# Third stage of a fused kernel: the outputs' sum and rounded part on GpSimd for two heads at a time, and reciprocals of two score tiles in one instruction

## What is computed

```python
def _L1_attn_ref(x, norm_scale, split_scale, Wq, Wk, Wv, Wo):
    ...
    nrm = jnp.linalg.norm(x, axis=-1, keepdims=True) * d ** (-0.5)
    h = norm_scale * x / (nrm + EPS) * split_scale
    q = (h @ Wq.T).reshape(b, s, H, dh)
    k = (h @ Wk.T).reshape(b, s, G, dh)
    v = (h @ Wv.T).reshape(b, s, G, dh)
    ...
    scores = jnp.einsum('bghsd,bgtd->bghst', q, k) / np.float32(np.sqrt(dh))
    attn = jax.nn.softmax(scores, axis=-1)
    out = jnp.einsum('bghst,bgtd->bghsd', attn, v)
    out = out.reshape(b, H, s, dh).transpose(0, 2, 1, 3).reshape(b, s, H * dh)
    return x + out @ Wo.T
...
x = L0_attn_x
x = x + _layernorm(_L0_attn_ref(_layernorm(x, axis=-1)), axis=-1)
x = x + _layernorm(_L0_ffn_ref(_layernorm(x, axis=-1), L0_ffn_factors, L0_ffn_bias), axis=-1)
x = x + _layernorm(_L1_attn_ref(_layernorm(x, axis=-1), ...), axis=-1)
x = x + _layernorm(_L1_ffn_ref(_layernorm(x, axis=-1), ...), axis=-1)
```

## Time and profile before

| what | value |
|---|---|
| time, median of 3 runs | 1461.83 us (1461.3 to 1461.9) |
| the profiled execution's time | 1460.45 us |
| its span in the profile | 1458.6 us |
| PE busy | 1386.4 us, 95% of the span |
| DVE busy | 1010.8 us, 69% |
| ACT busy | 798.1 us, 55% |
| POOL busy | 740.7 us, 51% |
| mean granted clock of PE | 0.989 |

### The profile page before, as it was taken

The page is one execution under the profiler, slowest core; times in us unless marked ns, Lnnn a source line. Parts: engine busy times, 40 slices in busy tenths (PEclk is TensorE's granted clock), DMA queues, the critical chain, the costliest instruction groups (busy, mean ns, idle before and its releaser), DMA issues.

```text
span 1458.6 us, 20717 instructions
## 1 busy us (share of the span) xinstructions
PE 1386.4 (95%) x6864; PEld 1134.4 (78%) x6864; DVE 1010.8 (69%) x2070; ACT 798.1 (55%) x1554; POOL 740.7 (51%) x1008
## 2 busy tenths in 40 slices
PE   5999999988999999999999999799999999999996
PEld 4888877766777877878787887588888888888884
DVE  5888869867989898989898989666242442434333
ACT  4666646647777878786868788632222222213221
POOL 5888646735536465554646455553343424333241
PEclk9999999999999999999999999999999999999998
DMA  6665133241302112121212041430101011010100
GB/s 192 169 174 127 40 101 116 87 130 38 94 4 64 65 44 88 44 87 37 87 28 96 15 121 40 145 138 1 58 1 59 4 54 58 0 58 0 58 29 29
DMA packets 53516, 101.32 MB, mean 69 GB/s; under 512 B 3760, under 2 KB 4784, under 8 KB 53424
## 3 DMA queue, kind: packets, MB, share of 16 engines
q1 hardware_dynamic: 49728, 92.83, 19.1%
q0 software_dynamic: 3696, 7.34, 3.1%
HBM read 70.79 MB, written 25.17 MB: 66 GB/s over the span
## 4 chain that ended last, share of the span: by engine, by line
PE 75%; DVE 13%; POOL 4%; issue 4%; ACT 3%; DMA 1%; SPq 0%; POOLq 0%; DVEq 0%; ACTq 0%
PE context L1889 13%; PE score L2367 11%; PE context L2367 11%; PE context L58 6%; PE score L58 6%; PE context L2395 5%; PE turned L2395 5%; PE score L899 4%; PE turned L1925 4%; PE context L1951 2%; PE context L1953 2%; DVE g_neg_max L1754 2%; PE context L1925 2%; DVE g_q L1677 1%; DVE g_ptl L1770 1%
## 5 line engine op out<-in xcount | busy, mean ns | idle before, releaser
L1413 POOL TENSOR_SCALAR g_prob<-g_prob,g_inv_sum 128x512 f32<-128x512 f32 x256 | 178.0, 697 | 268.9 <-DVE g_inv_sum L1759 268.8
L1548 ACT ACTIVATE g_prob<-score,g_neg_max 128x512 f32<-128x512 f32 x256 | 177.2, 692 | 115.5 <-DVE g_neg_max L1754 113.1
L2143 POOL TENSOR_TENSOR f_hl<-f_hidden,f_hh 128x512 fp32r<-128x512 f32 x88 | 121.9, 1386 | 216.0 <-DVE f_hh L2276 216.0
L1754 DVE TENSOR_REDUCE g_neg_max<-score 128x1 f32<-128x512 f32 x256 | 174.7, 682 | 43.9 <-PE score L58 43.4
L2367 PE MATMUL context<-g_hth,f_w 128*128 128x512 f32 x352 | 137.8, 391 | 2.3 <-ACT f_w L2193 2.2
L2367 PE MATMUL score<-g_hth,f_w 128*128 128x512 f32 x352 | 137.8, 392 | 0.6 <-DVE g_htl L2293 0.5
L2367 PE MATMUL context<-g_htl,f_w 128*128 128x512 f32 x352 | 137.1, 390 | 0.0
L2367 PE MATMUL score<-g_htl,f_w 128*128 128x512 f32 x352 | 137.1, 390 | 0.0
L58 PE MATMUL score<-g_kh,g_q 128*128 128x512 f32 x256 | 123.4, 482 | 10.7 <-ACT g_prob L1548 7.5
L2199 ACT ACTIVATE f_silu<-score,g_bits 128x512 f32<-128x512 f32 x44 | 30.3, 690 | 176.1 <-PE score L2367 176.1
L2199 ACT ACTIVATE f_silu<-context,g_bits 128x512 f32<-128x512 f32 x44 | 30.4, 690 | 174.5 <-PE context L2367 174.5
(11 more groups left out here) (261 smaller groups left out, 3950.6 us busy)
## 6 DMA issues: line engine op xcount, KB each, us to landing
xt<-x_t SPq DMA_DIRECT2D x16, 512.0 KB, 6.9
x_mixed<-x_resident SPq DMA_DIRECT2D x8, 1024.0 KB, 4.4
x_pair<-x_mixed SPq DMA_DIRECT2D x8, 1024.0 KB, 8.2
g_res<-x_mixed SPq DMA_DIRECT2D x8, 1024.0 KB, 6.5
x_attended<-g_res SPq DMA_DIRECT2D x8, 1024.0 KB, 5.1
x_pair<-x_attended SPq DMA_DIRECT2D x8, 1024.0 KB, 5.6
x_resident<-x SPq DMA_DIRECT2D x7, 1024.0 KB, 11.3
factor_sum<-factors POOLq DMA_DIRECT2D x7, 1024.0 KB, 10.8
```

Source lines behind the costliest of these rows:

```text
L1413: nc.gpsimd.tensor_scalar(prob[:, at, :], prob[:, at, :], inv_sum[:, at:at + 1], 1.0, ALU.mult, ALU.mult).then_inc(prob_ready, 1)
L1548: nc.scalar.activation(prob[:, at, :], score[u % 2][:, :], ACT.Exp, bias=neg_max[:, at:at + 1], scale=1.0, accum_out=row_sum[:, at:at + 1] ...
L1754: nc.vector.reduce_max(neg_max[:, at:at + 1], score[u % 2][:, :], AX, negate=True).then_inc(max_ready, 1)
L2143: self.nc.gpsimd.tensor_tensor(self.hl[:, at, :], self.hidden[:, at, :], self.hh[:, at, :].bitcast(F32), ALU.subtract).then_inc(self.hl_re ...
```

## The change

It does three things in the third stage.

1. ACT copies both halves of the output bank to SBUF, into out_parts, two copies of 64 x 512 for each head (parts_of in place of v_lo_of). The bank is free for PE after that (part_ready in place of sum_ready).
2. POOL adds the two parts for two heads in one instruction of 128 x 512 (sum_of, in the steps SUM_AT = 15, 23, 31, 39) and makes the high part itself (hi_of_output), followed in the same step by the low part. CONVERT becomes (26, 27, 32, 39). DVE no longer has sums or casts.
3. DVE takes the reciprocals of two tiles in one instruction, in even steps only, for tiles u - 2 and u - 1. POOL normalises both in the even step.

```diff
-SUM_LAG = OUT_LAG + 2
+SUM_AT = tuple(OUT_LAG + T + 2 + 2 * T * m for m in range(T))
...
-CONVERT = (25, 26, 32, 39)
+CONVERT = (26, 27, 32, 39)
...
-    g.v_lo_part = sb("v_lo_part", [DH, 2, N])
+    g.out_parts = sb("out_parts", [P, 2, N])
...
+            def sum_of(b, m):
+                pool.wait_ge(part_ready, b * HEADS + 2 * m + 2)
+                pool.wait_ge(ol_ready, b * T + m + 1)
+                nc.gpsimd.tensor_tensor(out_sum[:, m, :], out_parts[:, 0, :], out_parts[:, 1, :],
+                                        ALU.add).then_inc(sum_ready, 1)
+
+            def hi_of_output(b, m):
+                pool.wait_ge(sum_ready, b * T + m + 1)
+                if b == 0 and m == 0:
+                    pool.wait_ge(s.mixed_stored[6], 16)
+                    pool.wait_ge(s.mixed_stored[B - 1], 16)
+                if b > 0 and m == 0:
+                    pool.wait_ge(side_ready, side_use(b, "wo3") + 1)
+                nc.gpsimd.tensor_copy(oh[:, m, :], out_sum[:, m, :]).then_inc(oh_ready, 1)
+
             def lo_of_output(b, m):
                 pool.wait_ge(oh_ready, b * T + m + 1)
-                if b == 0 and m == 0:
-                    pool.wait_ge(s.mixed_stored[B - 1], 16)
...
-                if u > 0 or not first:
-                    if not drain or u == 0:
-                        normalise(b * UNITS + u - 1, u + 3)
+                if u % 2 == 0 and (u > 0 or not first):
+                    normalise(b * UNITS + u - 2, u + 2)
+                    normalise(b * UNITS + u - 1, u + 3)
...
+                for m, at in enumerate(SUM_AT):
+                    if at == u and not drain:
+                        sum_of(b, m)
+                    if at - UNITS == u and not first:
+                        sum_of(b - 1, m)
                 for m, at in enumerate(CONVERT):
-                    if at + 1 == u and not drain:
+                    if at == u and not drain:
+                        hi_of_output(b, m)
                         lo_of_output(b, m)
...
-            def v_lo_of(head, hd):
-                act.wait_ge(out_ready, head + 1)
-
-                nc.scalar.copy(v_lo_part[:, hd % 2, :], output[HALF[1], :]).then_inc(part_ready, 1)
+            def parts_of(b, hd):
+                if hd % 2 == 0 and b + hd > 0:
+                    act.wait_ge(sum_ready, b * T + hd // 2)
+                act.wait_ge(out_ready, b * HEADS + hd + 1)
+                for part, half in enumerate(HALF):
+                    last = nc.scalar.copy(out_parts[HALF[hd % 2], part, :], output[half, :])
+                last.then_inc(part_ready, 1)
...
-                if (u > 0 or not first) and (not drain or u == 0):
-                    at = (u - 1) % 4
+                if u % 2 == 0 and (u > 0 or not first) and (not drain or u == 0):
+                    at = (u - 2) % 4
                     dve.wait_ge(exp_ready, g)
-                    nc.vector.reciprocal(inv_sum[:, at:at + 1], row_sum[:, at:at + 1]).then_inc(inv_ready, 1)
+                    nc.vector.reciprocal(inv_sum[:, at:at + 2], row_sum[:, at:at + 2]).then_inc(inv_ready, 2)
...
-                            pe.wait_ge(sum_ready, b * HEADS + hd)
+                            pe.wait_ge(part_ready, b * HEADS + hd)
```

More of the change, by code:

```diff
@@ L1245, in grouped_attention @@
         kh, kl, v, pth, ptl, oh, ol = own.kh, own.kl, own.v, own.pth, own.ptl, own.oh, own.ol
-        v_lo_part, xn, v_turned = own.v_lo_part, own.xn, own.v_turned
+        out_parts, xn, v_turned = own.out_parts, own.xn, own.v_turned
         x, prob, total, out_sum, feature = s.x_pair, s.prob, s.total, s.out_sum, s.feature
@@ L1466, in step @@
                     output_weights_lo(OUTPUT_WEIGHTS.index(u - 1))
+                for m, at in enumerate(SUM_AT):
[3 more added lines that the diff above has]
+                        sum_of(b - 1, m)
                 for m, at in enumerate(CONVERT):
-                    if at + 1 == u and not drain:
+                    if at == u and not drain:
+                        hi_of_output(b, m)
                         lo_of_output(b, m)
-                    if at + 1 - UNITS == u and not first:
+                    if at - UNITS == u and not first:
+                        hi_of_output(b - 1, m)
                         lo_of_output(b - 1, m)
@@ L1494, in _ @@
             step(B, 0, 0, False, True, True)
-            lo_of_output(B - 1, 2)
             residual(B - 1, (B - 1) % 2, 0)
             residual(B - 1, (B - 1) % 2, 1)
+            sum_of(B - 1, 3)
+            hi_of_output(B - 1, 3)
             lo_of_output(B - 1, 3)
@@ L1607, in step @@
                 if done % T == 0 and not (first and done < 0) and not (drain and done >= 0):
-                    v_lo_of(b * HEADS + done // T, done // T)
+                    parts_of(b + done // UNITS, done // T % HEADS)
                 if u in NORM and not first:
@@ L1703, in total_of @@
                     last.then_inc(ostats, 1)
[L1705 to L1718, removed]
             def mixed_of(t):
@@ L1774, in step @@
                         total_of(b - 1, side_use(b, name), int(name[2]))
[L1775 to L1784, removed]
                 if not last and not drain and u in STEP_PIECES[b]:
@@ L1818, in _ @@
             gated.hi_of_hidden(dve, 0, 0, 1, True)
-            step(B, 0, 7, False, True, True)
             gated.low_tile(dve, 2)
@@ L1994, in last_steps @@
                 gated.down_of(pe, 0, 0, 0, with_lo, (
-                    (sum_ready, B * HEADS), (lo_ready, B * UNITS),
+                    (part_ready, B * HEADS), (lo_ready, B * UNITS),
                     (side_free, side_use(B, "wo2") + 1), (side_free, side_use(B, "wo3") + 1)))
```

## The result

The changed kernel takes 1470.36 us (median of six runs, 1468.48 to 1471.5), the kernel before 1461.87 us beside it (six runs, 1461.3 to 1464.11). The ratio is 1.0056, with a 95% interval of 1.0043 to 1.0069: slower, inside both ranges of the prediction and 3.6 us under its number. The profiled execution of the changed kernel took 1469.95 us with a span of 1468.1 us.

The account below looks back on a forecast made before the run. PE was taken to set the pace; 11.1 + 0.55 + 1.4 + 0.7 - 1.0 - 0.5 = +12.2 us on the profiled 1460.45 gave 1472.7, with 1.4 for the median 1474 us; own range 1468 to 1481, whole range 1463 to 1487.

Parts of the forecast that it names:

- GpSimd's queue to tile 26: POOL at batch boundaries: casts and low parts delay tile 26, so PE waits 1.36 us in step 30.
- v: PE's turn of v, behind late tile 26 and ACT's second copy: 1.85 us later per boundary, 11.1 us for six.
- The exponential of tile 8: ACT's copy in step 6 delays the exponential PE awaits by 0.2 us, seven times: 1.4 us.
- DVE's relief: Sums, casts and reciprocals leaving DVE shorten PE's waits by 0.07 us a batch, 0.5 us in all.
- Batch 0: First batch: 1.0 us gained as step 9's reciprocal wait goes; at its boundary only ACT's 0.55 us counts.
- The end of the stage: Last two heads' sum, cast and low part on POOL delay PE's last wo products 0 to 1.5 us; 0.7 taken.
- Busy times: Third stage: DVE busy some 78 us less, POOL 65 to 70 more, ACT 37 more.
- That only ACT's copies show: Rival: PE finds tile 26 ready, v is 0.4 us late seven times; +3.4 us, 1465 us; chance 0.10.
- That DVE had set the pace: Rival: three PE waits released by DVE end, up to 7.1 us go, 1.0 in batch 0; 1454 us; chance 0.07.
- The dear cast: Rival: POOL's cast costs as much as a two-input operation, 1.33 us; +26 us, 1488 us; chance 0.13.

Follow-up runs that it names:

- e3: The changed kernel with its four casts a batch back on DVE, the last one a step later (step 40); 1464.52 us, ratio 1.0029.
- e4: The changed kernel with casts and low parts of three of a batch's four blocks moved to steps 32, 36 and 37; 1462.02 us, ratio 1.0009.
- e2: The kernel before with only the pairing of reciprocals and normalisations; sums and casts on DVE, one copy on ACT; 1458.64 us, ratio 0.9984.
- e8: The kernel before with only ACT's second copy of the output, read by nobody; sums stay on DVE; 1477.09 us, ratio 1.0110.
- e1: The changed kernel without the pairing: one reciprocal and one normalisation in every step, as before; 1472.54 us, ratio 1.0085.
- e5: The changed kernel with ACT copying the turned v ahead of step 30's output copies; 1469.44 us, ratio 1.0057.
- e7: The kernel before with the pairing, and the turned v copied ahead of step 30's output part on ACT; 1454.74 us, ratio 0.9954.
- e9: The changed kernel with late casts, first block in step 34, turned v copied first on ACT, third sum in step 32; 1452.63 us, ratio 0.9947.

## Why the prediction was right, and where it was not

- **GpSimd's queue to tile 26: right.** 1.36 us predicted (the prediction's own times, 620.88 less 619.54, make it 1.34), 1.34 measured by PE's starts (1.15 in the row of waits, which begins at the modelled end of the instruction ahead). From the start of tile 24 to the end of tile 26 the queue took 7.9 us (614.92 to 622.8), against 8.02. It lay some 0.4 us earlier in the batch than predicted, and so did PE, both through the relief below, so that the wait came out as if neither had moved. The cast was 0.61 us, not 0.70; with its own wait the low part starts 0.69 behind it (616.23 to 616.92), not 0.74. ol 0 took 1.31. e3 and e4 show that these casts and low parts are the cause.
- **v: right.** From the turn of tile 26 to that of v 5.11 us (622.87 to 627.98), 5.08 predicted. A boundary costs 1.86 us (-0.38 to +1.48), against 1.85.
- **The exponential of tile 8: right**, +0.20 us. The visible wait shrank from 0.35 to 0.21 all the same, since 0.28 us of the lateness comes one instruction earlier, at the turn of tile 6, which GpSimd normalises in step 8. The mechanism is ACT's: in e2, with the pairing and one copy, the same 0.28 us at tile 6 leaves nothing at the score. Its price is less sure, for in e8 the second copy beside single reciprocals cost 0.07 us.
- **DVE's relief: the step that was mis-sized.** "I take 0.07 us a batch": measured 0.5 to 0.55. The reciprocal's wait in step 9 is there in every batch, 0.29 us, and PE's wait behind it, 0.36 us, doesn't appear among the waits. Six batches at 0.46 us are 2.8 us, the better part of the 3.6 by which I was high. e1, which has no relief there, and e2, which has all of it, show that it belongs to the pairing.
- **Batch 0: better than predicted, through something not in the prediction**: -1.44 us with its boundary, against -0.25 (0.55 + 0.2 - 1.0). The granted clock makes the difference. PE, 350 to 356 us, the kernel before, then the changed one:

```profile
350.00:356.00 6.00, 4.79 (x18) 3.75 (x17) 4.41 (x10) 5.34 (x12) 2.05 (x3) 0.72 0.00 0
```

```profile
350.00:356.00 6.00, 4.77 (x28) 3.79 (x26) 5.21 (x10) 5.80 (x15) 1.98 (x3) 1.00 0.00 0
```

  Before, PE's products follow each other at 0.43 us there (from 352.39 to 354.52), which is the lower of the clock's two levels (1.2 and 2.4 GHz), and after at 0.23, the higher. It had waited 0.69 and 1.21 us for exponentials shortly before the fall, in the changed kernel 1.23 once. From the score at 351.80 to the next one, at 355.23, PE took 3.43 us; the same instructions take 1.86 in the changed kernel. That is 1.57 us, more than the whole gain of batch 0. Ahead of it PE was 0.97 us in front, near the 1.0 predicted, and behind it 1.1 us were lost again. In the profiles of all eight kernels with the pairing this stretch reads 1.00, in the three without (before, e1, e8) 0.72; each was profiled once.
- **The end of the stage: right in size by luck**, +0.83 us with what follows it, against 0.7. The prediction had PE wait longer for the last low part on GpSimd. In the changed kernel it doesn't wait for it at all, where it waited 0.73 us before:

```profile
956.06 1.29 POOL L1433 TENSOR_TENSOR g_ol<-g_out_sum,g_oh 128x512 fp32r<-128x512 f32 x1
957.58 0.39 PE L2365 MATMUL context<-g_htl,f_w 128*128 128x512 f32 x1
957.81 0.40 PE L1887 MATMUL turned<-g_woh,g_oh 128*128 128x512 f32 x1
```

  PE is late there with its own products of the fourth stage, which wait for weights that ACT rounds when their transfer has landed. Before, then after:

```profile
943.54 0.50 PE L2367 MATMUL context<-g_hth,f_w 128*128 128x512 f32 x1 [2.17 <-ACT f_w L2193]
```

```profile
952.43 0.50 PE L2365 MATMUL context<-g_hth,f_w 128*128 128x512 f32 x1 [3.83 <-ACT f_w L2191]
```

  Counted from the last turn of v, PE comes to this wait 1.5 us ahead of the kernel before and leaves it 0.2 us behind. Of the sixteen products that follow, seven then start 0.43 us ahead of the next one, where before they follow each other at 0.23: another 1.6 us. The 0.73 us waited before go against that. The weights' low part on DVE had not ended either, as the prediction took it to: the sum beside it took 1.65 us instead of 1.29. I did not take this place apart by a run.
- **+0.74 us before the first turn of v** were not predicted and are not of the change. In the eleven profiles that turn begins between 320.1 and 322.4 us, behind code that all share; a single profile is no better than that.
- **Busy times: too large.** DVE 54 us less in the whole kernel (1010.8 to 956.6), not 78; POOL 55 more, not 65 to 70; ACT 32 more, not 37. I had multiplied durations, but an instruction's last 0.07 to 0.1 us overlaps with the next one's start and is counted once.
- **The rivals.** That only ACT's copies show: refuted by e3 and e4. Its price, +3.4 us, is not far from what these two cost with GpSimd's queue relieved, 4.2 and 1.7 us. The 16 us of e8 are the copies' price with the sums still on DVE, in another kernel. That DVE had set the pace: refuted as put, but e2 shows a piece of it. The dear cast: refuted, it takes 0.61 us.

## What to carry to other kernels

GpSimd was 62% busy and yet full for 23 us at a stretch, and there a removed wait only moved to the next consumer of its queue (e5); where it had slack, the same edit paid (e7). So lay PE's starts of two kernels side by side, find the whole stretch without idle time, and move work out of it, as e9 does, before removing waits beside it. A move is worth what it takes out of waiting chains, not what it takes off the busy time: one reciprocal of 0.16 us that waited for ACT cost 0.5 us a batch, and while it stood there, the loss of eight sums and four casts a batch on DVE won PE nothing (e1). Short waits hide in the modelled end of the instruction ahead, so compare the times from start to start, and not only the waits. And a sum that comes out right can hold terms that don't: look at each place before trusting the size, as at the stage's end here.

## What the runs showed of the hardware

A cast on DVE and an operation on GpSimd lengthen each other where they meet. In e3_casts_dve, GpSimd and then DVE:

```profile
611.79 1.53 POOL L1413 TENSOR_SCALAR g_prob<-g_prob,g_inv_sum 128x512 f32<-128x512 f32 x2 [4.15 <-DVE g_inv_sum L1765]
```

```profile
612.20 0.56 DVE L1724 CAST g_oh<-g_out_sum 128x512 fp32r<-128x512 f32 x1
```

The pair of normalisations takes 1.39 us right behind (at 617.83), the cast 0.43 (at 614.75) in the same kernel. With all casts on GpSimd the 32 low parts there take 1.29 to 1.31 us each. Before, the eight that met a cast of 0.56 us on DVE took 1.46 to 1.48, and one beside the low part of the weights (1.75 us on DVE) took 2.73. *The Trainium skill, Advanced Engine Details and Errata, section VectorE Performance Modes, says that GpSimd's instructions and those of DVE that use both of its ports interfere with and block each other*; by that rule, the trace agrees as far as these numbers go, and the 1.30 that the prediction used for ol 0 came out at 1.31.

A cast of 128x512 from f32 to fp32r is the cheapest GpSimd operation of its size here: 0.61 us against 0.70 for the normalisation and 1.29 to 1.32 for two inputs.
